# Index stage of a graph network: row statistics taken for two node tiles at a time

## The reference, cut to what matters

```
x = x + gnn0(layernorm(x), src, dst, gamma, beta, W, b)     # 3 graph convolutions
x = x + ffn0(layernorm(x), W_router, W_up, W_down, ...)     # 32 experts, top-k
x = x + gnn1(layernorm(x), edges, edge_attr_8, Wq, Wk, ...) # attention over edges
x = x + ffn1(layernorm(x), router_w, w1, w2, ...)           # 8 experts, top-2
```

## Time and profile before

| | |
|---|---|
| median of 3 runs | 3785.86 us (3785.84 to 3785.95) |
| the profiled execution | 3788.61 us, its span 3786.9 us, so 1.7 us lie around the span |
| index phase | from about 6 us to 281.26 us of the span |
| busy over the span | TensorE 86%, VectorE 64%, ScalarE 36%, GpSimd 33% |

### The profile page before, as it was taken

The page is one execution under the profiler, slowest core; times in us unless marked ns, Lnnn a source line. Parts: engine busy times, 40 slices in busy tenths (PEclk is TensorE's granted clock), DMA queues, the critical chain, the costliest instruction groups (busy, mean ns, idle before and its releaser), DMA issues. The chain is left out here.

```text
span 3786.9 us, 61965 instructions
## 1 busy us (share of the span) xinstructions
PE 3244.4 (86%) x18244; PEld 2741.1 (72%) x18245; DVE 2435.9 (64%) x6053; ACT 1369.5 (36%) x2564; POOL 1242.0 (33%) x1606
## 2 busy tenths in 40 slices
PE   5855889997775329999999999999969995969999
PEld 1213667776775319999999999999858884847676
DVE  7865877644776764555455455545368886957776
ACT  4632655422111424445444444444311111124443
POOL 4763532222553012223222322232233320035552
PEclk9977999998555559999999999999989997989999
DMA  4305323334996033444444444453321111156663
GB/s 157 102 20 131 107 90 124 99 124 144 316 308 210 6 80 99 135 140 113 127 108 141 108 127 125 126 135 104 79 78 55 56 55 53 72 124 162 156 155 99
DMA packets 256000, 449.66 MB, mean 119 GB/s; under 512 B 70818, under 2 KB 76307, under 8 KB 255367
## 3 DMA queue, kind: packets, MB, share of 16 engines
q1 hardware_dynamic: 182065, 280.74, 22.4%
q0 software_dynamic: 62368, 145.38, 17.6%
q10 hardware_dynamic: 11318, 20.54, 1.4%
HBM read 319.46 MB, written 126.83 MB: 118 GB/s over the span
## 5 line engine op out<-in xcount | busy, mean ns | idle before, releaser
L1519 PE MATMUL experts_psU<-experts_x_hi,experts_up_hi 128*128 128x312 f32 (+1 forms) x1408 | 442.9, 315 | 21.1 <-issue 14.9
L1548 PE MATMUL experts_psY<-experts_hid_hi,experts_dn_hi 128*128 128x312 f32 (+1 forms) x1408 | 438.8, 312 | 0.0
L1520 PE MATMUL experts_psU<-experts_x_lo,experts_up_hi 128*128 128x312 f32 (+1 forms) x1408 | 436.5, 310 | 0.0
L1521 PE MATMUL experts_psU<-experts_x_hi,experts_up_lo 128*128 128x312 f32 (+1 forms) x1408 | 435.9, 310 | 0.0
L1549 PE MATMUL experts_psY<-experts_hid_lo,experts_dn_hi 128*128 128x312 f32 (+1 forms) x1408 | 430.8, 306 | 0.0
L1550 PE MATMUL experts_psY<-experts_hid_hi,experts_dn_lo 128*128 128x312 f32 (+1 forms) x1408 | 429.7, 305 | 0.0
L1478 POOL DMA_INDIRECT experts_xg<-xn,experts_token_i x96 | 129.8, 1352 | 596.9 <-DVE experts_token_i L1656 577.4
L1694 DVE TENSOR_TENSOR experts_hid_lo<-experts_hid,experts_hid_hi 128x312 fp32r<-128x312 f32 (+1 forms) x352 | 161.4, 480 | 252.0 <-ACT experts_hid L1611 252.0
L1609 ACT ACTIVATE experts_hid_hi<-experts_psU,experts_bup 128x312 fp32r<-128x312 f32 (+1 forms) x352 | 183.7, 522 | 320.5 <-PE experts_psU L1521 319.1
L1519 PEld LDWEIGHTS experts_psU<-experts_x_hi,experts_up_hi 128*128 128x128 f32 (+1 forms) x1408 | 265.3, 188 | 22.6 <-issue 20.5
L1686 DVE TENSOR_TENSOR experts_dn_lo<-experts_dn_raw,experts_dn_hi 128x1536 fp32r<-128x1536 f32 (+1 forms) x128 | 207.9, 1624 | 100.4 <-ACT experts_dn_hi L1587 100.3
(11 more groups left out here) (469 smaller groups left out, 8051.2 us busy)
## 6 DMA issues: line engine op xcount, KB each, us to landing
experts_dn_raw<-in_L_ffn_W_down SPq DMA_DIRECT2D x96, 768.0 KB
conv<-gcn_diff SPq DMA_DIRECT2D x120, 256.0 KB, 2.9
all_stage<-in_L_ffn_W_up SPq DMA_DIRECT2D x32, 682.5 KB, 6.9
index_xt<-in_x SPq DMA_DIRECT2D x78, 256.0 KB, 2.8
route_xt<-in_x SPq DMA_DIRECT2D x78, 256.0 KB, 4.6
x<-route_xt SPq DMA_DIRECT2D x78, 256.0 KB, 4.5
xn<-route_xn ACTq DMA_DIRECT2D x78, 256.0 KB, 4.7
two_xt<-x SPq DMA_DIRECT2D x78, 256.0 KB, 2.8
```

The lines of the kernel that those rows point to most:

```text
L1519: pe.matmul(acc, up_hi[:, c, cols], x_hi[:, c, :], start=(c == 0), stop=False)
L1520: pe.matmul(acc, up_hi[:, c, cols], x_lo[:, c, :], start=False, stop=False)
L1521: mm = pe.matmul(acc, up_lo[:, c, cols], x_hi[:, c, :], start=False, stop=(c == C - 1))
L1548: pe.matmul(acc, dn_hi[0:w, m, cols], hid_hi[0:w, m, :], start=(m == 0), stop=False)
```

## The change

`stats` is called once for two tiles. It issues both `bn_stats`, then both `bn_aggr`, then one addition of eps for both variances and one new multiplication of both means by -1 (into a fourth column of `mv`); a wait stands before each `bn_aggr` for its own `bn_stats`, and one before the addition for both `bn_aggr`. GpSimd's `root` runs once for two tiles: one power of 128 x 2 and one product of 128 x 2 (`tensor_tensor` in place of `tensor_scalar`), after both tiles' statistics. ScalarE's wait for `rooted` is for the pair. The last tile, 78, forms a pair of one. The assertion on the constants, not shown, asks for even AHEAD and R and an odd number of tiles.

```diff
-        mv = ph.sb("mv", [P, R, 3])
+        mv = ph.sb("mv", [P, R, 4])
...
-                act.wait_ge(rooted, 2 * n + 2)
+                act.wait_ge(rooted, n // 2 * 2 + 2)
...
-            def root(n):
+            def root(p):
+                n, w = 2 * p, min(2, NT - 2 * p)
                 r, j = node_rows(g, n), n % R
-                pool.wait_ge(stat_step, 3 * n + 3)
+                pool.wait_ge(stat_step, 6 * p + 2 + 2 * w)
                 if n >= R:
-                    pool.wait_ge(normed, n - R + 1)
+                    pool.wait_ge(normed, n - R + w)
                 pool.sem_inc(waited, 1)
-                pool.tensor_tensor(rstd[0:r, j:j + 1], mv[0:r, j, 2:3], g.minus_half[0:r, 0:1], ALU.pow).then_inc(rooted, 1)
-                pool.wait_ge(rooted, 2 * n + 1)
+                pool.tensor_tensor(rstd[0:r, j:j + w], mv[0:r, j:j + w, 2], g.minus_half[0:r, 0:w], ALU.pow).then_inc(rooted, 1)
+                pool.wait_ge(rooted, 2 * p + 1)
                 pool.sem_inc(waited, 1)
-                pool.tensor_scalar(shift[0:r, j:j + 1], mv[0:r, j, 0:1], -1.0, rstd[0:r, j:j + 1],
-                                   ALU.mult, ALU.mult).then_inc(rooted, 1)
+                pool.tensor_tensor(shift[0:r, j:j + w], mv[0:r, j:j + w, 3], rstd[0:r, j:j + w], ALU.mult).then_inc(rooted, 1)
...
-                for n in reached(t, 0):
-                    root(n)
+                for n in reached(t, 0)[::2]:
+                    root(n // 2)
...
-            chain = Chain(v, stat_step, 3)
+            chain = Chain(v, stat_step)
 
             def stats(n):
+                p, w = n // 2, min(2, NT - n)
                 r, j = node_rows(g, n), n % R
-                v.wait_ge(loaded[j], 16 * (n // R + 1))
                 if n >= R:
-                    v.wait_ge(rooted, 2 * (n - R) + 2)
-                chain.at(n)
-                layer_norm(v, chain, xt[0:r, j, :], st[:, j, :], mv[:, j, :], r, waited)
-                chain.end()
+                    v.wait_ge(rooted, n - R + 2)
+                for k in range(w):
+                    v.wait_ge(loaded[j + k], 16 * (n // R + 1))
+                    v.sem_inc(waited, 1)
+                    chain.go(v.bn_stats(st[0:r, j + k, :], xt[0:r, j + k, :]))
+                for k in range(w):
+                    chain.wait(6 * p + 1 + k)
+                    v.sem_inc(waited, 1)
+                    chain.go(v.bn_aggr(mv[0:r, j + k, 0:2], st[0:r, j + k, :]))
+                chain.wait(6 * p + 2 * w)
+                chain.go(v.tensor_scalar(mv[0:r, j:j + w, 2], mv[0:r, j:j + w, 1], EPS, None, ALU.add))
+                chain.go(v.tensor_scalar(mv[0:r, j:j + w, 3], mv[0:r, j:j + w, 0], -1.0, None, ALU.mult))
...
-                for stat in reached(t, 0):
+                for stat in reached(t, 0)[::2]:
                     stats(stat)
```

More of the change, by code:

```diff
@@ L190, in index_and_stats @@
     R, S, G, AHEAD, LAG = 12, 6, 4, 12, 4
-    assert FULL * ET == E and NT <= 2 * ET + AHEAD and ET % G == 0 and 5 * NH <= 512 and EP < 1 << 15
+    assert AHEAD % 2 == R % 2 == 0 and NT % 2 == 1 and FULL * ET == E and NT <= 2 * ET + AHEAD and ET % G == 0 and 5 * NH <= 512 and EP < 1 << 15
     with Phase(nc, "index") as ph:
@@ L333, in scatter @@
                                             rec[:, t, :], None).then_inc(scattered, 16)
-            for n in range(AHEAD):
-                root(n)
+            for p in range(AHEAD // 2):
+                root(p)
             for t in range(ET):
-                for n in reached(t, 0):
-                    root(n)
+                for n in reached(t, 0)[::2]:
+                    root(n // 2)
                 if t >= G:
@@ L440, in _ @@
                 v.sem_inc(hot, 1)
-                for stat in range(n * AHEAD // 2, (n + 1) * AHEAD // 2):
+                for stat in range(n * AHEAD // 2, (n + 1) * AHEAD // 2, 2):
                     stats(stat)
```

## The result

The changed kernel takes 3757.39 us (median of 4 runs, 3756.16 to 3761.35) against 3785.85 for the kernel before: a ratio of 0.992, 95% interval 0.9909 to 0.9932. The medians differ by 28.5 us, and the interval of the ratio reaches from 25.7 to 34.5 us.

A forecast was written before the change was run, and what follows sets the result against it. GpSimd's last scatter was taken to end the index phase, with VectorE pacing both engines after the change. Round 32's root 23.5 us earlier plus 0.80 for that pair made 24.3 us off 3785.86, so 3761.5 us; range 3756 to 3772.

The forecast's parts named there:

- start of round 0's first `bn_stats`: Before the index loop: VectorE gets there 1.2 us earlier (bounds 0.9 and 1.5), limited by its wait for TensorE.
- rounds 0 to 31 on VectorE: Index loop up to round 32's first `bn_stats`: 32 pairs at 0.62 us each save 19.8 us.
- round 32, `bn_stats` to power: GpSimd's power in round 32 starts 2.12 us after VectorE's first `bn_stats`, instead of 4.59.
- that power to the hand-over: After round 32's power: 0.80 us saved on that pair itself, GpSimd's closed queue of grades and scatters unshortened.
- Which engine ends the phase: End of the index phase: GpSimd comes last, 13.8 us behind VectorE; both engines must become faster to end it earlier.
- a pair saves 0.62: VectorE's statistics for two tiles: 1.87 us instead of 2.49, saving 0.62 us (bounds 0.40 and 0.66).
- duration less 0.08: VectorE: a step without a wait for its forerunner costs its duration less 0.08 us, taken from last-phase rows.
- GpSimd's pair: GpSimd from first power to first scatter: 1.63 us instead of 2.43, saving 0.80 us (0.54 at the low end).
- The drained pipeline: VectorE steps cost their whole duration even unwaited: a pair saves 0.33 us, 14.7 in all, 3771 us; chance 0.11.
- TensorE takes over: TensorE at a lower clock paces the loop, 19.4 us per four rounds; 6.4 us go back, 3768 us; chance 0.07.
- GpSimd held by VectorE's comparisons: Shared SBUF interfaces slow the loop's power and product: from no change to 26 us slower, 3812 us; chance 0.06.
- Given back later: TensorE's clock falls elsewhere in the 3500 us behind the phase, losing the gain: 3775 to 3790 us; chance 0.06.

The follow-up runs named there:

- b0: The kernel before, unchanged, run again on a third chip: 3795.24 us in its one profiled execution, 3790.23 as the median of its other runs there.
- a1: The changed kernel, unchanged, run again on the third chip beside the kernel before: 3756.89 us, ratio 0.9917 to the kernel before.
- e1: Changed kernel with GpSimd's power and shift one tile at a time again, VectorE's interleaving kept: 3786.15 us, ratio 0.9986 to the kernel before.
- e2: Changed kernel with VectorE tile after tile, waiting behind each instruction, GpSimd's paired root kept: 3791.82 us, ratio 1.0003 to the kernel before.
- e3: Changed kernel with two GpSimd powers of one column in place of one of two: 3772.3 us, ratio 0.995 to the kernel before.
- e4: Changed kernel with a wait behind each of the pair's two `tensor_scalar`: 3772.72 us, ratio 0.9952 to the kernel before.
- e5: Changed kernel with four tiles at a time every second round in the loop, on both engines: 3757.44 us, ratio 0.9912 to the kernel before.
- e7: Changed kernel with a wait behind each `bn_stats`: 3773.88 us, ratio 0.9954 to the kernel before.

## Why the forecast was right in kind and short in size

Its terms against the two pairs of traces, each from the same marks (the earlier trace rows for the first):

| term of the forecast | forecast | first traces | b0 and a1 |
|---|---|---|---|
| start of round 0's first `bn_stats` | 1.2 | 58.37-57.46 = 0.91 | 57.35-56.31 = 1.04 |
| rounds 0 to 31 on VectorE | 19.8 | 168.21-145.30 = 22.91 | 167.80-143.74 = 24.06 |
| round 32, `bn_stats` to power | 2.47 | 4.59-2.10 = 2.49 | 4.55-2.11 = 2.44 |
| that power to the hand-over | 0.80 | 50.09-48.91 = 1.18 | 49.91-48.93 = 0.98 |
| sum | 24.3 | 27.49 | 28.52 |

**Which engine ends the phase: right.** From round 4 the two engines were 2% apart, and the halves alone moved the hand-over by 3.8 and -1.0 of the 27.5 us (e1, e2); put back on either engine, a cost is paid (e3, e4). The offset of the power is right to 0.02.

**The step that failed is the size of VectorE's pair: "a pair saves 0.62", with 0.66 as its upper bound.** It saves 0.71. I split the new pair into the right five steps, and four of them came out a little shorter than I put them: `bn_stats` to `bn_stats` 0.59 for 0.61, to the second `bn_aggr` 0.84 for 0.84, to the addition 0.21 for 0.22, to the multiplication 0.08 for 0.09, to L485 0.06 for 0.09, and the 0.02 for two more increments was not there at all. My price, "duration less 0.08", came from two rows of another phase; here it is duration less 0.09 or 0.10. It is not that a step with nothing between is always that short: in the same round L515 follows L513 with no wait between, 0.32 after a start of 0.40, so less 0.08. Why these steps differ by 0.02 no run shows. Small errors of one sign, times 32, make 0.09 x 32 = 2.9 us.

**One stall that I counted as kept went away too.** In round 27 of the kernel before, the timeline of the first trace reads:

```profile
196.38 0.81 ACT L274 ACTIVATE index_xn<-index_xt,index_shift,index_rstd 128x512 f32<-128x512 f32 x1 [2.49 <-POOL index_shift L315]
...
197.25 1.63 PE L354 MATMUL index_psN<-index_xn,all_ones 128*1 128x512 f32 x2 [2.81 <-ACT index_xn L274]
198.67 1.92 PE L356 MATMUL index_psQ<-index_xsq,all_ones 128*1 128x512 f32 x2
200.38 1.30 PE L354 MATMUL index_psN<-index_xn,all_ones 128*1 128x512 f32 x2
201.52 1.02 PE L356 MATMUL index_psQ<-index_xsq,all_ones 128*1 128x512 f32 x2
202.47 0.52 PE L402 MATMUL index_psL<-index_tabs,index_pick 128*128 128x240 bf16 x4
...
203.03 0.41 DVE L505 TENSOR_TENSOR index_prod<-index_psL,index_is_hi 128x240 f32<-128x240 f32 x1 [1.42 <-PE index_psL L402]
```

GpSimd, by then well behind, delivers `shift` late; ScalarE idles 2.49 for it and TensorE 2.81 for ScalarE. TensorE's next pairs of summing matmuls take up to 1.92 instead of 1.02, in a window (185 to 205) with a granted clock of 0.91, so in part at 1.2 GHz. Its look-up is late, and VectorE waits 1.42. In none of the three traces of the changed kernel does VectorE wait there; where GpSimd lags again (e1, e3), such waits are back, and in the runs where it does not lag (e2, e4, e5, e7) VectorE waits for TensorE nowhere between 80 and 200 us. With it, rounds 0 to 31 close: on the third chip 32 x 0.71 + 1.18 = 23.9 of 24.06. In the first traces 1.48 us have to be taken off, since that execution of the changed kernel waited so long in round 1:

```profile
65.97 0.41 DVE L513 TENSOR_TENSOR index_prod<-index_psL,index_is_hi 128x240 f32<-128x240 f32 x1 [1.48 <-PE index_psL L402]
```

TensorE had idled 2.02 and 0.79 just before, and its pairs then took 1.87 to 1.92. The other two traces show nearly the same idle times, but shorter stretches of long pairs and no such wait. 22.7+1.4-1.5 = 22.6 of 22.91. So the shortfall of the forecast, 3.2 us in the first traces, is 2.9 from the pair, 1.4 from the stall and 0.4 from behind round 32, less 1.5 for the wait in round 1 and 0.3 before the loop; 0.3 is left over.

**Before the loop: right in size, for a reason that held by half.** The root of tiles 4 and 5 fell beside the comparisons, as said:

```profile
31.59 3.76 POOL L313 TENSOR_TENSOR index_rstd<-index_mv,all_minus_half 128x2 f32<-128x2 f32 x1 [7.55 <-DVE index_mv L427]
35.52 4.85 POOL L316 TENSOR_TENSOR index_shift<-index_mv,index_rstd 128x2 f32<-128x2 f32 x1 [0.18 <-POOL index_rstd L313]
```

The matmuls of the second end covered it. VectorE then waited for TensorE, which was only slightly earlier: 0.91 and 1.04, near the lower bound of 0.9.

**GpSimd's pair: 0.84 for 0.80.** One sum of the forecast is wrong, without effect on its result: with the low saving of 0.54 GpSimd would need 21.50-4 x 0.54 = 19.3 per four rounds, not 18.7.

**Behind round 32: 1.2 and 1.0 for 0.80.** The paired root alone gave 0.98 of it in the first traces: from its start to the `grade` 233.38-231.17 = 2.21 before, 206.09-204.86 = 1.23 now.

**The rivals.** *The drained pipeline* is refuted by the rows of round 10: instructions of 0.17 follow each other after 0.08 and 0.06, and the `bn_stats` after 0.59, not 0.69. The Trainium skill, VectorE: DVE Perf Modes, section "The DRAIN you can't avoid", has it that an instruction waits for the pipeline of the one before to empty with or without semaphores between them; by that e4 should have cost next to nothing, and it cost 0.27 a pair, so here the measurement decides against it. The same section of the Trainium skill adds that a next instruction that is not held starts earlier, and the rows agree with that.

*TensorE takes over* did not happen from 80 us on: it was busy 18.8 of 20 us at a clock of 1.00. It did happen for one round at the start of the loop: the clock was 0.88 from 60 to 80 us, and that is where VectorE lost the 1.48 of round 1; in the other two traces the same window reads 0.96 and 1.00, with no such wait.

*GpSimd held by VectorE's comparisons* did not come in at its size: products of 0.19, and powers of 0.73 to 0.91 in the loop. Not every power starts beside L485 and L508, as the forecast had it: 8 of the 29 in rounds 4 to 32 start beside L508, as those of rounds 4 and 32 above, and take 0.80 to 0.91, the others 0.73 or 0.74. That is at most 0.2 a pair, where the rival needed 0.9; in e2, where most start beside the same two instructions, it is 0.74 at most, so what makes the difference stays open. Before the loop the rows above show the contention that the Trainium skill describes (GPSIMD Engine Reference, section "Specifications"), 3.76 us for a power of 0.74.

*Given back later* did not happen: 3504.2 to 3505.8 us behind the hand-over in three traces of the changed kernel, 3505.6 in the first of the kernel before.

**Open.** On the other two chips the medians differ by 31.8 and 33.3 us, and the phase explains 28.5 of the 33.3 (b0 and a1). In b0 the part behind the hand-over is 3793.5-279.61 = 3513.9, 8 us longer than in the first trace of the same kernel, half of it in one load of weights in the last phase (9.02 us instead of 4.92). Why the kernel before is longer there on these chips no run here settles, and I claim nothing of it for the change.

## What to carry to other kernels

Where two engines hand work to each other each round and are within a few per cent, compare their own paces per period before any sum: shortening one alone moves the wait (e1, e2), and afterwards a tenth on either is paid in full or nearly so (e3, e4, e7). An instruction's wait for its forerunner on the same engine is worth naming in hundredths and removing by interleaving independent work, because a loop multiplies it, errors in its price included. And an engine that lags, even one that seems only to queue, can cost the leader a stall by a long way round: look in the old trace for single waits that hang on the lag before counting them as kept.

## What the runs showed of the hardware

- VectorE: a wait for the instruction right before costs 0.13 us behind a `tensor_scalar` of 0.17 (0.20 against 0.07) and 0.27 behind a `bn_stats` of 0.69 (0.86 against 0.59). Unwaited, the next starts 0.08 to 0.10 before the end of the one before. Behind a waited `bn_aggr` of 0.18 the addition starts after 0.22, a `bn_stats` in e2 after 0.36.
- GpSimd: a power took 0.55 for one column, 0.74 for two (0.88 to 0.91 in some rounds), 1.04 to 1.25 for four (e5) and 1.63 for eight, each of 128 partitions: 0.14 to 0.2 for a further column on some 0.4. Two powers of one column in succession took 1.09 to 1.12 in most rounds (e3).
- TensorE: an idle time of 2.81 us in the middle of the loop was followed by matmul pairs of up to 1.92 instead of 1.02 us, and VectorE waited 1.42 for what came behind them.
